# A pre-norm decoder layer on one core: other units between the links of the norms, residuals summed on TensorE, outputs sent by ScalarE

## The reference, cut to what matters

```python
x = x + attn(layernorm(x))        # 16 heads of 16; causal (q.k)**2 weights, divided by their sum; @ Wo
x = x + align(ctx, layernorm(x))  # distances of 77 context rows to 1024 tokens, cheapest monotone
                                  # path (dynamic time warping), each context row added along its path
x = x + ffn(layernorm(x))         # 256 -> 1024, ten butterfly stages, gelu, ten stages, 1024 -> 256, biases
```

## Time and profile before

| | us |
|---|---|
| runs | 899.43, 904.36, 904.51 |
| median | 904.36 |
| profiled execution | 906.11 |
| its span | 904.4 |

### The profile page before, as it was taken

The page is one execution under the profiler, slowest core; times in us unless marked ns, Lnnn a source line. Parts: engine busy times, 40 slices in busy tenths (PEclk is TensorE's granted clock), DMA queues, the critical chain, the costliest instruction groups (busy, mean ns, idle before and its releaser), DMA issues.

```text
span 904.4 us, 12060 instructions
## 1 busy us (share of the span) xinstructions
PE 777.9 (86%) x3927; PEld 381.4 (42%) x3927; DVE 493.9 (55%) x1913; ACT 448.0 (50%) x678; POOL 158.0 (17%) x340
## 2 busy tenths in 40 slices
PE   4898987789899978979989988868899950999998
PEld 3353323234333334323334322444386640658667
DVE  5636553541546123597998894266779886430000
ACT  1246775776667655768776777422412200241220
POOL 2221232221221111212332212011013000200100
PEclk9898987899999998979999999788899985899999
DMA  4481532210323221213431223000110013000001
GB/s 147 166 244 58 187 117 71 70 52 20 117 64 146 78 59 27 64 51 118 150 105 48 75 63 59 1 8 2 40 40 32 16 34 74 13 0 24 24 0 47
DMA packets 53146, 61.29 MB, mean 68 GB/s; under 512 B 21391, under 2 KB 32323, under 8 KB 53083
## 3 DMA queue, kind: packets, MB, share of 16 engines
q1 hardware_dynamic: 51995, 56.32, 20.6%
q0 software_dynamic: 1088, 4.19, 1.5%
HBM read 37.17 MB, written 23.32 MB: 67 GB/s over the span
## 4 chain that ended last, share of the span: by engine, by line
PE 62%; DVE 19%; ACT 7%; DMA 4%; issue 4%; SPq 2%; POOL 0%; ACTq 0%; DVEq 0%
PE psO L1299 13%; PE psS L1282 13%; PE psS L1446 9%; PE psW L1456 8%; PE psW L1351 5%; PE psW L1374 3%; ACT ARENA L866 3%; DVE FOLD L1072 3%; PE psW L1342 2%; DVE STATS L1127 2%; PE psW L1358 2%; PE psW L1383 2%; PE psW L1436 2%; SPq L613 2%; DVE FOLD L1012 2%
## 5 line engine op out<-in xcount | busy, mean ns | idle before, releaser
L866 ACT ACTIVATE ARENA<-psS 128x1024 f32<-128x1024 f32 (+3 forms) x384 | 300.7, 811 | 113.4 <-PE psS L1282 110.4
L1282 PE MATMUL psS<-ARENA 96*128 96x512 bf16 (+3 forms) x768 | 197.3, 348 | 29.1 <-ACT ARENA L866 28.1
L780 POOL TENSOR_SCALAR_AFFINE_SELECT ARENA<-ARENA 128x256 f32<-128x256 f32 x256 | 111.2, 438 | 417.3 <-ACT ARENA L866 415.1
L1299 PE MATMUL psO<-ARENA 128*32 128x512 f32 (+3 forms) x1536 | 173.1, 524 | 2.7 <-ACT ARENA L871 2.5
L1282 PEld LDWEIGHTS psS<-ARENA 96*128 96x128 bf16 x768 | 57.1, 100 | 218.6 <-ACT ARENA L866 124.5
L1456 PE MATMUL psW<-W2E,ARENA 128*128 128x256 f32 x512 | 111.8, 379 | 0.7 <-ACT ARENA L887 0.4
L1456 PEld LDWEIGHTS psW<-W2E,ARENA 128*128 128x128 f32 x512 | 96.7, 189 | 16.4 <-issue 1.4
L940 ACT ACTIVATE ARENA<-psS,BEFF 128x512 f32<-128x512 f32 x64 | 43.4, 687 | 89.7 <-PE psS L1446 89.7
L1174 DVE TENSOR_TENSOR X<-X,psW 128x512 f32<-128x512 f32 x32 | 21.9, 688 | 97.1 <-PE psW L1374 52.2
L1351 PE MATMUL psW<-XX,ARENA 128*128 128x512 f32 x128 | 67.6, 635 | 5.0 <-DVE ARENA L1162 3.0
L1446 PE MATMUL psS<-XX,MIXA 128*128 128x512 f32 x128 | 58.4, 611 | 3.4 <-ACT ARENA L940 2.7
(11 more groups left out here) (145 smaller groups left out, 814.5 us busy)
## 6 DMA issues: line engine op xcount, KB each, us to landing
ARENA<-qk_parts SPq DMA_DIRECT2D x192, 128.0 KB, 2.7
qk_parts<-ARENA SPq DMA_DIRECT2D x16, 768.0 KB, 3.5
out<-ARENA SPq DMA_DIRECT2D x16, 256.0 KB, 2.1
X<-in_x POOLq DMA_DIRECT2D x3, 1024.0 KB, 7.3
dist<-ARENA SPq DMA_DIRECT2D x1, 2560.0 KB, 8.2
MORE<-dist SPq DMA_DIRECT2D x16, 160.0 KB, 2.2
path<-MORE SPq DMA_DIRECT2D x16, 80.0 KB, 2.0
path<-FOLD SPq DMA_DIRECT2D x16, 80.0 KB, 2.1
```

What stands on the lines that cost most here:

```text
L780: pool.affine_select(out=blk, in_=blk, compare_op=ALU.is_ge, fill=0.0, base=0, pattern=[[0, 2], [1, P]], channel_multiplier=-1).then_inc(s ...
L866: nc.scalar.activation(A[:, (2 * G + a) % A_PAIRS, :, 0:N], psS[:, a, :, 0:N], ACT.Square).then_inc(s_sq, 1)
L1282: ins = nc.tensor.matmul(psS[:, a, j, 0:N], KST[0:STACK, g % 2, 2 * a + j, kt * P:(kt + 1) * P], QST[0:STACK, g % 2, 2 * a + j, q0:q0 + N] ...
L1299: ins = nc.tensor.matmul(psO[32 * j:32 * j + 32, o % 2, q0 - qc * HALF:q0 - qc * HALF + N], V1[:, kt, GH * g + j], A[:, (2 * G + j // 2) % ...
```

## The change

Fill: in all four attention batches and behind the last one, real units lie between stats, variance, root and `rstd` of each norm, where pauses or nothing lay; the student norm of batch 2 is done in halves; in batch 0, `mix` and `qk(1)` alternate, and `qk(1, 5..7)` alternates with `chain(1)`. The norm of the feed-forward of batch 1 is spread over the units between attention and `warp(1)`, with its second `along` pair moved ahead. The feed-forward norms of batches 0 and 1 use the second set of statistics buffers.

Residual: for batches 0 and 1, each token tile's sum on TensorE begins with the identity times `X` and a row of ones times the bias; `base(0)`, `base(1)` and GpSimd's sums go. ScalarE copies the result and issues its DMA.

Distances: each way's distances have a semaphore of their own, the way that the first rows need is computed and sent first, and the first load waits for it alone. Elsewhere waits are rewritten for these semaphores.

```diff
@@ -41,7 +41,7 @@
-LEAD, LAST, AHEAD, SOON = 5, 8, 5, 4
+LEAD, LAST, AHEAD, SOON = 6, 8, 5, 4
@@ -199,10 +199,6 @@
-    mixes = pairs(0, 8) + pairs(0, 9) + [("bias",)]
-    down = ([("w1", i) for i in range(4)] + chain(1) + pairs(1, 9) + pairs(1, 8) + pairs(1, 7)
-            + [("down", i) for i in range(HT // 2)])
-
     def steps_of(b):
@@ -214,19 +210,32 @@
+    context, order = [("context", i) for i in range(B)], [("order", i) for i in range(B)]
+    w1 = [("w1", i) for i in range(4)]
     side = [("qk", 0, i) for i in range(8)]
     links = chain(0)
...
     plan = norm_units("x", 0, 0) + [("bits",)] + turns(0) + [("coef", i) for i in range(3)] + side[:4]
     plan += flat([a, c] for a, c in zip(side[4:] + values(0)[:3], links)) + values(0)[3:] + wexp + both(0)
-    for b, fill, due in ((0, up + [("context", i) for i in range(B)] + [("order", i) for i in range(B)] + front(1) + mixes + down, {}),
-                         (1, values(1)[:2] + wo(0)[:2] + values(1)[2:] + wo(0)[2:] + front(2) + back(0), {**value_due(1), **wo_due(0)})):
-        steps = steps_of(b)
-        if b == 0:
-            plan += flat(spread(steps[:-3], fill)) + flat(steps[-3:-1])
-        else:
-            plan += flat(spread(steps[:-8], fill, due)) + flat(spread(steps[-8:-1], half_back(1, 0)))
-        plan += both(b + 1) + steps[-1]
+    norm_x = lambda b: norm_units("x", b)
+    qk = lambda b: [("qk", b, i) for i in range(8)]
+    two = lambda a, b: flat([x, y] for x, y in zip(a, b))
+
+    nx, links = norm_x(1), chain(1)
+    fill = (up + context + nx[:4] + order + nx[4:5] + pairs(0, 8)[:2] + nx[5:6] + pairs(0, 8)[2:] + nx[6:] + turns(1)
+            + two(qk(1), pairs(0, 9)) + [("bias",)] + qk(1)[4:5] + w1 + two(links, qk(1)[5:]) + links[3:]
+            + pairs(1, 9) + pairs(1, 8) + pairs(1, 7) + [("down", i) for i in range(HT // 2)])
+    steps = steps_of(0)
+    plan += flat(spread(steps[:-3], fill)) + flat(steps[-3:-1]) + both(1) + steps[-1]
+
+    nx, ns0, v, w = norm_x(2), norm_units("student", 0), values(1), wo(0)
+    fill = (v[:2] + w[:2] + nx[:4] + v[2:3] + nx[4:5] + v[3:] + nx[5:6] + w[2:3] + nx[6:] + w[3:] + ns0[:4] + turns(2)
+            + qk(2)[:2] + ns0[4:5] + qk(2)[2:4] + ns0[5:6] + qk(2)[4:6] + ns0[6:] + qk(2)[6:] + [("pause",)] * 3
+            + [("turn_s", 0, 0), ("turn_s", 0, 1), ("dist", 0, 0)])
+    steps, hb = steps_of(1), half_back(1, 0)
+    plan += flat(spread(steps[:-8], fill, {**value_due(1), **wo_due(0)}))
+    plan += flat(spread(steps[-8:-1], hb[:5] + [("turn_s", 0, 2), ("turn_s", 0, 3)] + hb[5:6] + [("dist", 0, 1)] + hb[6:]))
+    plan += both(2) + steps[-1]
@@ -246,22 +255,26 @@
-    steps = steps_of(2)
-    third = (spread(steps[:LEAD], values(2)[:2] + half_back(1, 1), value_due(2))
-             + spread(steps[LEAD:-8], values(2)[2:] + front(3), {u: n - LEAD for u, n in value_due(2).items()})
+    steps, nx, v, hb = steps_of(2), norm_x(3), values(2), half_back(1, 1)
+    third = (spread(steps[:LEAD], v[:1] + hb[:5] + v[1:2] + hb[5:9] + v[2:3] + hb[9:], value_due(2))
+             + spread(steps[LEAD:-8], nx[:4] + v[3:] + nx[4:5] + [("pause",)] * 3 + nx[5:6] + [("pause",)] + nx[6:] + [("pause",)] * 3
+                      + turns(3) + qk(3), {u: n - LEAD for u, n in value_due(2).items()})
...
-    steps = steps_of(3)
-    fourth = spread(steps[:-LAST], values(3)[:2] + wo(2)[:2] + values(3)[2:] + wo(2)[2:] + back(2), {**value_due(3), **wo_due(2)})
+    steps, v, h0, h1 = steps_of(3), values(3), half_back(2, 0), half_back(2, 1)
+    fourth = spread(steps[:-LAST], v[:2] + h0[:4] + v[2:3] + h0[4:5] + v[3:] + h0[5:6] + h1[:1] + h0[6:9] + h1[1:4] + h0[9:11] + h1[4:5]
+                    + h0[11:] + h1[5:9] + [("pause",)] * 3 + h1[9:], {**value_due(3), **wo_due(2)})
...
-    (measure, finish), both_tiles = whole_norm("ffn", "turn_f", 1), along(1)
-    plan += flat(spread(steps[-LAST:-1], half_back(3, 0) + half_norms("ffn", "turn_f", 0, along(0), 0) + both_tiles + measure)) + steps[-1]
-
-    second = warp(1)
+    (sa, na), (sb, nb) = half_parts("ffn", "turn_f", 0, 1)
+    a, hb, other, along_other = along(0), half_back(3, 0), norm_units("ffn", 1), along(1)
+    plan += flat(spread(steps[-LAST:-1], hb[:5] + a[2:] + hb[5:9] + sa[:3] + a[:1] + sa[3:] + hb[9:11] + a[1:2] + na[:3] + hb[11:] + sb[:3]
+                        + na[3:] + sb[3:] + nb + along_other[2:] + other[2:4])) + steps[-1]
+
...
-    ahead = half_back(3, 1)
-    plan += ahead[:2] + early_hidden[:SOON - 1] + ahead[2:-1] + early_hidden[SOON - 1:] + ahead[-1:] + finish
-    plan += [("gelu",) + u[1:] for u in early_hidden] + [("base", 0)]
-    pieces = singles(hidden(0, 0)[SOON:] + hidden(0, 1) + outs(0, 0) + outs(0, 1) + [("base", 1)] + hidden(1, 0) + hidden(1, 1) + outs(1, 0))
+    ahead = half_norm("student", "turn_s", 3, 1, [], [("dist", 3, 1)])
+    plan += along_other[:2] + wo(3)[2:3] + other[:2] + ahead[:1] + wo(3)[3:] + early_hidden[:SOON - 1] + ahead[1:7] + other[4:6]
+    plan += ahead[7:-1] + early_hidden[SOON - 1:] + ahead[-1:] + other[6:] + [("turn_f", 1, i) for i in range(4)]
+    plan += [("gelu",) + u[1:] for u in early_hidden]
+    pieces = singles(hidden(0, 0)[SOON:] + hidden(0, 1) + outs(0, 0) + outs(0, 1) + hidden(1, 0) + hidden(1, 1) + outs(1, 0))
@@ -316,7 +327,7 @@
     def later(what, b):
...
-        return 1 if (what, b) == ("ffn", 1) else 0
+        return 1 if what == "ffn" and b < PAIR else 0
@@ -614,14 +624,14 @@
             def dist_out(b, h):
...
-                sp.wait_ge(s_dn, b * 2 + h + 1)
...
-                for way in range(WAYS):
+                for n, way in enumerate((h, 1 - h)):
                     blocks = slice(0, MID) if h == way else slice(MID, W_BLK)
+                    sp.wait_ge(s_dn, 2 * (b * 2 + h) + n + 1)
...
-                                 BACK[b][3][rows_of(way)].rearrange("p (w c) -> p w c", c=CB)[:, blocks]).then_inc(s_dist_out[b][h], 16)
+                                 BACK[b][3][rows_of(way)].rearrange("p (w c) -> p w c", c=CB)[:, blocks]).then_inc(s_dist_out[b][h][way], 16)
@@ -651,8 +661,8 @@
                 if k < 2:
                     for i in range(PAIR):
                         for h in range(2):
-                            sp.wait_ge(s_dist_out[PAIR * w + i][h], 16 * WAYS)
-                    if w:
+                            sp.wait_ge(s_dist_out[PAIR * w + i][h][h if k == 0 else 1 - h], 16)
+                    if w and k == 0:
@@ -692,11 +702,9 @@
                 elif kind == "out":
                     _, b, i = u
-                    if on_both(b, i):
-                        sp.wait_ge(s_added, added_of[b, i] + 1)
-                    else:
+                    if not on_both(b, i):
...
-                    sp.dma_start(out[b].rearrange("(t p) d -> p t d", p=P)[:, 2 * i:2 * i + 2], OUTB[:, i % 2]).then_inc(s_out[i % 2], 16)
+                        sp.dma_start(out[b].rearrange("(t p) d -> p t d", p=P)[:, 2 * i:2 * i + 2], OUTB[:, i % 2]).then_inc(s_out[i % 2], 16)
@@ -789,24 +797,17 @@
-                            pool.wait_ge(s_dist_out[b - 1][h], 16 * WAYS)
+                            for way in range(WAYS):
+                                pool.wait_ge(s_dist_out[b - 1][h][way], 16)
...
-                elif kind == "out" and on_both(*u[1:]):
-                    _, b, i = u
-                    pool.wait_ge(s_free[bank(*u)], made(*u))
-                    if i == 0:
-                        pool.wait_ge(s_base, b + 1)
-                    pool.tensor_tensor(out=OUTB[:, i % 2], in0=OUTB[:, i % 2], in1=XB[:, 2 * i:2 * i + 2], op=ALU.add).then_inc(s_added, 1)
                 elif kind == "base":
                     b = u[1]
-                    if b and on_both(b - 1, 0):
-                        pool.wait_ge(s_added, max(added_of[b - 1, i] for i in range(TT // 2)) + 1)
-                    elif b:
+                    if b == PAIR:
+                        pool.wait_ge(s_o_read, B * NO)
+                    else:
...
-                    if b == 0:
-                        pool.wait_ge(s_xn, normal_of["student", B - 1, TT // 2 - 1] + 1)
...
                     pool.wait_ge(s_bias, 1)
                     pool.tensor_tensor(out=XB, in0=X[:, b], in1=BIAS[:].unsqueeze(1).to_broadcast([P, TT, D]), op=ALU.add
@@ -888,18 +890,19 @@
                 elif kind == "dist":
...
-                        act.wait_ge(s_dist_out[b - 1][0], 16 * WAYS)
-                        act.wait_ge(s_dist_out[b - 1][1], 16 * WAYS)
+                        for way in range(WAYS):
+                            act.wait_ge(s_dist_out[b - 1][0][way], 16)
+                            act.wait_ge(s_dist_out[b - 1][1][way], 16)
...
-                        act.wait_ge(s_dn, b * 2 + h)
+                        act.wait_ge(s_dn, 2 * (b * 2 + h))
                     nc.scalar.activation(DSQ[0:SPAN], psW[0:SPAN, bank(*u)], ACT.Relu, bias=AA[:, b:b + 1]
...
-                    nc.scalar.activation(DN[rows_of(0), EDGE + h * HALF:EDGE + (h + 1) * HALF], DSQ[rows_of(0)], ACT.Sqrt)
```

(19 more changed lines are left out.)

20 lines of the change are left out of this document (10 added, 10 removed).

## The result

| | us |
|---|---|
| runs of the kernel before beside it | 899.43, 899.96, 904.36, 904.51; median 902.16 |
| runs of the changed kernel | 861.68, 863.13, 864.07, 866.80; median 863.6 |
| ratio | 0.9577 [0.9531, 0.9623] |
| profiled execution after | 866.8, span 865.1, clock 0.970 |

The forecast was 862.3 (842 to 885). Faster by 4.2%: the forecast's own case. The sum came out well because errors of both signs met, so the parts are taken one by one.

What follows compares the result with a forecast made beforehand. TensorE, 86% busy, loses time idling or slow in attention and waiting 32.3 us for VectorE's second-alignment chain. From 906.11 us, tail -21.5 and attention -20.6 give 864.0; less 1.8 to the median, 862.3 us (842 to 885).

Steps and rivals of the forecast that it cites:

- the tail behind attention: Everything from attention's end to the kernel's end: forecast -21.5 us in all.
- The chain (a, b): VectorE's second alignment: no wait for a late load, -5.5 us; no hold-up by GpSimd's sums and `base(1)`, -10.1 us.
- (a): Second alignment: with outputs gone from SyncE's queue, loads of distances no longer wait behind them, -5.5 us.
- Rival 5: A load still stands behind something on SyncE, such as path transfers: +5.5, 868 us; chance inside the forecast's 0.68.
- The start (c): Between attention and the second alignment's first row: fewer statistics ahead, earlier first distances, -4.4 us (bounds 0 and -7).
- TensorE's pieces: TensorE's work beside the second alignment: seven outputs grow 1.74 us each, 12.2 us (9.2 to 18.3), hidden, ending at 744.1.
- (a) to (c): The three savings on the second alignment's chain: it ends 20.0 us earlier, so TensorE could go on at 747.4.
- rival 3: TensorE bounds the tail: one-row matmuls at double cost, chain 3 us earlier; resumption 17 us earlier, 865 us; inside 0.68.
- Behind the wait: From TensorE's resumption after the path to the first `hidden`: `along` at full clock, 14.8 us for 16.3, -1.5 us.
- Attention: Attention stretch: half of 28.3 us in ten idle times, -14.2, and a sixth of 38.5 lost to clock, -6.4: -20.6 us.
- Rivals 1, 2 and 4: Attention gives nothing (882.9 us, chance 0.18); nearly all, -47 (836 us, 0.10); norms' links too close, slower (917 us, 0.04).
- The signs that I named: Whole kernel: path wait below 8 us, scans near 0.30, GpSimd 19 us less, 64 more matmul records, roots below 2 us.

Runs made afterwards that it cites:

- `ways_together`: The changed kernel with both ways' distances computed in the old order, sent together and waited for together; 868.43 us, ratio 0.9616.
- `before_again`: The kernel before, no edit, profiled a second time; 901.99 us, ratio 1.0.
- `old_fill`: The changed kernel with the fill laid out as before, new outputs and distances way by way kept; 883.09 us, ratio 0.9792.

## Why the prediction was right, and where not

That the time came out 1.3 us from the forecast is partly luck. By the two traces the tail behind attention gave 15.3 us where 21.5 were forecast, and attention 24.0 where 20.6 were; against the second pair of traces attention gave 20.9. The mechanism of the chain held, the cost on TensorE did not, and attention gave its sum by another split.

**The chain (a, b): right, in sum and parts.** Forecast 5.5 + 10.1 = 15.6, measured 15.5. VectorE's four groups took 73.3 us with GpSimd's work and 62.8 without. Scans beside a sum and the `tensor_tensor` beside `base(1)` were the right rows. The lock over a whole instruction (the Trainium skill, "SBUF — State Buffer", section "SBUF: two separate sides") agrees with the variance that ended 0.03 us behind `base(0)`; by it 12.1 us stood here, and 10.5 were measured, nearer to the rows' 10.1. For (a), 5.5 is what the kernel before lost. The size depends on when the outputs come: with the longer outputs and the earlier chain of the new kernel the same queue costs 10.9. Without the move to ScalarE, about half of what the sums on TensorE give the chain would have gone back into this queue (waits of 11.0 us in place of 5.5). Rival 5 did not come.

**The start (c): -3.0 for -4.4.** `ways_together` gives 1.2 of it, where I had 1.1. The order of `wo(3)` and the norms gave the rest, 1.8, where I had 3.3. `wo(3)` takes 5.41 us where it took 5.49, so the 1.2 us for a better clock did not come; it waits 2.71 us where it waited 6.33.

**TensorE's pieces: mis-sized.** The step that failed is "a one-row matmul is in no row here; I take 0.436, as the columns are the same". It takes 0.82 us, near the upper bound. An output grew by 2.50 us and not 1.74; from `hidden` at 610.48 to `along` at 727.12 it is 116.6 us where 98.8 stood: +17.8, not +12.2. "TensorE would be the bound were (a) to (c) 4 us bigger" came the other way: (a) to (c) were 1.5 smaller and the work was 5.6 bigger. This is rival 3 in its outcome: counted from attention's end, `along` comes 16.3 us earlier, where the forecast had 20.0 and the rival 17. The rival's other condition, a chain 3 us earlier than forecast, did not hold; the size of the work alone was enough. Being the bound costs TensorE the 2.1 us between 7.4 and 5.3, and no more. Of those 2.1 us the forms of the bias over 128 rows save 1.5 to 2.1 and give back 1.0 behind the wait.

**Behind the wait: +1.0 for -1.5.** The half clock went, as forecast: `along` takes 3.89 us, not 6.70. But the output behind it takes 9.54 (732.40 to 741.94), not 8.7, and TensorE waits 1.39 us for VectorE's addition of `along`, a wait I had not listed. It was 0.36 us in the kernel before, where `along` itself ran longer:

```profile
774.52 7.19 PE L1456 MATMUL psW<-W2E,ARENA 128*128 128x256 f32 x32 [0.36 <-DVE X L1174]
```

**Attention: the size nearly right, the split wrong.** -20.6 forecast, -24.0 between two traces and -20.9 between the second pair (603.7 to 582.8). I had 14.2 from idle time and 6.4 from the clock. Measured against `before_again` it is 7.0 from idle time and 13.3 from busy time; against `old_fill`, which is the cleaner pair, 6.3 and 7.0. The ten idle times shrank by more than the half that I took. In the changed kernel five over 1.2 us are left that end behind a link of a norm or behind the mixing, at 94.9, 101.2, 131.3, 177.5 and 577.1 us, together 12.4 us where 28.3 stood. But I had taken the rest of the idle time as it was, and it grew from about 34 to 42 us, so TensorE keeps 54 to 56 us in all. The clock gave more than I had, though part of that is the spread between executions. The interleaving in batch 0 gave nothing that can be told. Rivals 1, 2 and 4 fall: attention gave neither nothing nor 47 us, and it did not grow.

**The signs that I named.** Right: scans near 0.30, no second wait for distances, GpSimd 20.9 us less (19 named), 64 records more. Wrong: roots of ScalarE below 2 us. In attention one still waits 3.59 us, at 560; another waits 14.66 us at 594.75, behind attention, where ScalarE had nothing else to do.

## What to carry to other kernels

When an order of queues is repaired in several places at once, look for the engine that is next: here 11 us of TensorE's work could be taken out again without a change in time, because the path was only 2 us ahead of TensorE and the wait for it cost clock. A DMA that depends on a late product does not belong in the queue that feeds the critical chain, and a longer product makes the stall longer (3.73 us where 0.18 stood). Where an operation is in no row of the trace, its upper bound is the number to plan with: if the step still hides there, it is safe.

## What was not expected of the hardware

- An fp32 matmul of one row and 256 columns costs 0.82 us where one of 128 rows costs 0.43. Its weights are not loaded ahead (load and matmul both at 634.19), and neither are those behind it.
- Behind a TensorE wait of 3.88 us the next eight matmuls ran mostly at half clock (6.59 us, granted clock 0.50 over the first 5.7; behind no wait 3.89 us, clock 1.00). So a TensorE that was the bound with no gap and a freer one with a gap of 4 us came out level.
- The same attention plan ran at a mean clock of 0.93 in two traces of one kernel and 0.96 in another kernel with the same idle time. With one layout of batch 0 it took 137.7 to 142.9 us from one execution to the next. An idle sum alone does not give the clock.
